# Embedding, attention and experts on one core: the last feature tile of the experts is laid out as a full 64+64 tile and a narrow one whose high and low weights are one stationary operand

## The reference

```python
sg = silu(einsum('bsd,fd->bsf', x, Wsg)); su = einsum('bsd,fd->bsf', x, Wsu)
shared_out = einsum('bsf,df->bsd', sg * su, Wsd)              # shared expert, 704 features
topk_scores, topk_idx = top_k(softmax(logits), 2)             # 8 experts, 2 per token
g = silu(einsum('bsd,efd->bsef', x, Wg)); u = einsum('bsd,efd->bsef', x, Wu)
out_e = einsum('bsef,edf->bsed', g * u, Wd)                   # 352 features per expert
return routed_out + shared_out                                # routed_out weighs out_e by the scores
```

## Time and profile before

| | |
|---|---|
| median of 3 runs | 1667.9 us (1666.66 to 1669.73) |
| profiled execution | 1669.39 us, span 1667.6 us, mean granted TensorE clock 0.984 |
| TensorE busy | 1562.7 us, 94% of the span |
| VectorE busy | 1142.2 us, 68% |
| ScalarE busy | 931.8 us, 56% |
| experts' matmuls | from 719.9 us to the end |

### The profile page before, as it was taken

One profiled execution on the slowest core, in us unless ns is written; L12 is line 12 of the kernel. 1 busy time (PEld: TensorE's weight loads), 2 busy tenths in 40 slices (PEclk: granted clock), 3 DMA queues, 4 the chain that ended last, 5 costly groups with the idle time before them and its releaser, 6 DMA issues.

```text
span 1667.6 us, 34456 instructions
## 1 busy us (share of the span) xinstructions
PE 1562.7 (94%) x11589; PEld 1363.9 (82%) x11652; DVE 1142.2 (68%) x2228; ACT 931.8 (56%) x1902; POOL 528.9 (32%) x517
## 2 busy tenths in 40 slices
PE   2699986999999999879999999999999999999997
PEld 1354544888888888779999999999999999999996
DVE  3588886799999998564434666666666666656665
ACT  4987774687888788532223555555555555522221
POOL 3344445233333422007701222222222221033433
PEclk9999999899999999789999999999999999999999
DMA  9899984122222211131111577777666777543365
GB/s 310 247 317 331 319 267 105 45 59 63 61 65 57 63 51 39 41 129 51 38 50 57 188 246 245 241 246 242 236 237 241 237 238 237 192 152 113 121 217 191
DMA packets 91922, 274.50 MB, mean 165 GB/s; under 512 B 12640, under 2 KB 13152, under 8 KB 91744
## 3 DMA queue, kind: packets, MB, share of 16 engines
q1 hardware_dynamic: 70688, 223.71, 39.3%
q0 software_dynamic: 19072, 45.97, 10.9%
q10 hardware_dynamic: 2112, 4.19, 0.8%
HBM read 228.14 MB, written 45.69 MB: 164 GB/s over the span
## 4 chain that ended last, share of the span: by engine, by line
PE 56%; DMA 1%; DVE 0%; POOL 0%; ACT 0%; issue 0%; POOLq 0%; DVEq 0%
PE up_ps L1338 12%; PE up_ps L1336 12%; PE up_ps L1337 12%; PE down_ps L1336 6%; PE down_ps L1337 6%; PE down_ps L1338 6%; PE xT_ps L1380 2%; DMA comb<-slot_rows,slot_i 0%; DVE H L1286 0%; DMA xr<-x_turned 0%; DVE xT_lo L1203 0%; POOL comb L1138 0%; ACT xT_hi L1153 0%; DVE H L1278 0%; PE route_ps L1332 0%
## 5 line engine op out<-in xcount | busy, mean ns | idle before, releaser
L1336 PE MATMUL up_ps<-xT_hi,w_hi 128*128 128x256 f32 (+1 forms) x1704 | 483.6, 284 | 8.5 <-DVE xT_lo L1203 8.5
L1338 PE MATMUL up_ps<-xT_hi,w_lo 128*128 128x256 f32 (+1 forms) x1704 | 480.8, 282 | 0.0
L1337 PE MATMUL up_ps<-xT_lo,w_hi 128*128 128x256 f32 (+1 forms) x1704 | 478.8, 281 | 0.0
L1336 PEld LDWEIGHTS up_ps<-xT_hi,w_hi 128*128 128x128 f32 (+1 forms) x1704 | 308.0, 181 | 10.0 <-DVE xT_lo L1203 8.6
L1337 PEld LDWEIGHTS up_ps<-xT_lo,w_hi 128*128 128x128 f32 (+1 forms) x1704 | 308.1, 181 | 1.2
L1338 PEld LDWEIGHTS up_ps<-xT_hi,w_lo 128*128 128x128 f32 (+1 forms) x1704 | 308.0, 181 | 0.0
L1208 DVE TENSOR_TENSOR w_lo<-w_stage,w_hi 128x1408 fp32r<-128x1408 f32 (+1 forms) x123 | 201.4, 1665 | 125.0 <-ACT w_hi L1158 124.8
L1130 POOL DMA_INDIRECT xr<-x_rows,slot_tokens x78 | 120.6, 1546 | 441.4 <-PE xT_ps L1380 362.1
L1185 ACT ACTIVATE h_hi<-h 128x256 fp32r<-128x256 f32 (+1 forms) x213 | 89.0, 418 | 240.4 <-DVE h L1301 240.4
L1181 ACT ACTIVATE act_g<-up_ps 128x256 f32<-128x256 f32 (+1 forms) x213 | 79.8, 374 | 182.3 <-PE up_ps L1338 179.6
L288 DVE TENSOR_TENSOR W<-W,norm_ps 128x1000 f32<-128x1000 f32 x128 | 147.2, 1191 | 43.9 <-PE norm_ps L364 35.7
(11 more groups left out here) (184 smaller groups left out, 2738.2 us busy)
## 6 DMA issues: line engine op xcount, KB each, us to landing
W<-table_t SPq DMA_DIRECT2D x32, 2000.0 KB, 14.9
w_stage<-packed SPq DMA_DIRECT2D x80, 704.0 KB, 6.4
w_stage<-packed SPq DMA_DIRECT2D x40, 768.0 KB, 5.2
slot_rows<-y_rows SPq DMA_DIRECT2D x39, 512.0 KB, 6.7
xr<-x_turned SPq DMA_DIRECT2D x32, 512.0 KB, 3.8
x_rows<-x SPq DMA_DIRECT2D x32, 256.0 KB
x_turned<-x2T SPq DMA_DIRECT2D x32, 256.0 KB, 2.5
out<-H SPq DMA_DIRECT2D x32, 256.0 KB, 3.8
```

The source lines that it names most:

```text
L1336: pe.matmul(out, a_hi, b_hi, start=first, stop=False)
L1337: pe.matmul(out, a_hi, b_lo, start=False, stop=False)
L1338: return pe.matmul(out, a_lo, b_hi, start=False, stop=last)
```

## The change

The 96 features of the last tile become 64 ("wide") and 32 ("narrow").

For the 64 wide features, gate and up columns stand side by side and form one stationary operand of 128 columns: 4 steps times 3 matmuls write all 128 partitions of `up_ps[2]`, columns 0 to 255 (gate in partitions 0 to 63, up in 64 to 127).

For the 32 narrow features, the high weights of gate and up (64 columns) and their low weights (64 columns) stand side by side in `w_split` and form one stationary operand of 128 columns. One matmul of it against the high rows gives high times high in partitions 0 to 63 and low times high in 64 to 127 of `up_ps[2]`, columns 256 to 511. The product of the high weights with the low rows is a second matmul with 64 stationary columns, into partitions 0 to 63 of the same place. It is issued between the 128-column ones.

The sum of the two partition halves and the products are then made by more, narrower instructions: ScalarE does silu on 64 partitions, a copy of the other 64 partitions of the narrow part, and a silu on 32 partitions; VectorE adds twice on 32 partitions and multiplies on 64 and on 32. The weights' high and low copies share one tile per buffer, and the low parts of pieces 0 and 1 take two instructions each instead of one. The host packs the columns in the new order; the loads keep their sizes.

The diff goes through the constants, the weight tiles, ScalarE's tiles (`act`), VectorE's low weights and tile 2 (`dve`), and TensorE's tile 2 (`pe`).

```diff
+WIDE, NARROW = 64, 32
+UP_ORDER = ((0, 128), (128, 128), (256, WIDE), (256 + WIDE, NARROW))
+LO_STEPS = (2, 2, 1)
...
-        w_hi = [sb(f"w_hi{i}", [P, PACKED], F32R) for i in range(2)]
-        w_lo = [sb(f"w_lo{i}", [P, PACKED], F32R) for i in range(2)]
+        w_split = [sb(f"w_split{i}", [P, 2 * PACKED], F32R) for i in range(2)]
...
+        up_hi = [u[:, :, 0:2 * ROUTED_F] for u in up_all]
+        up_narrow = [u[:, :, BOTH_FROM:BOTH_TO] for u in up_all]
+        up_lo = [u[:, :, BOTH_TO:K_COLS] for u in up_all]
...
+                    wide = WIDE if j == 2 else f
+                    act.activation(act_g[0:wide, j, :], up_ps[j][0:wide, 0:BLOCK], ACT.Silu).then_inc(silu_done, 1)
+                    if j == 2:
+                        act.activation(act_g[WIDE:P, j, :], up_ps[j][WIDE:P, BLOCK:2 * BLOCK], ACT.Copy).then_inc(silu_done, 1)
+                        act.wait_ge(tail_added, n * 2 + 1)
+                        act.activation(act_g[WIDE:f, j, :], act_g[WIDE:f, j, :], ACT.Silu).then_inc(silu_done, 1)
+                    act.wait_ge(h_done, n * 4 + j + 1 + j // 2)
...
+                    dve.tensor_tensor(up_lo[buffer][:, k, :], whole[:, :, 0:BOTH_FROM], hi[:, :, 0:BOTH_FROM], ALU.subtract).then_inc(w_lo_done[piece], 1)
+                    dve.tensor_tensor(up_narrow[buffer][:, k, 2 * NARROW:4 * NARROW], whole[:, :, BOTH_FROM:2 * ROUTED_F],
+                                      hi[:, :, BOTH_FROM:2 * ROUTED_F], ALU.subtract).then_inc(w_lo_done[piece], 1)
...
+                        dve.tensor_tensor(act_g[WIDE:f, j, :], act_g[WIDE:f, j, :], up_ps[j][0:NARROW, BLOCK:2 * BLOCK],
+                                          ALU.add).then_inc(tail_added, 1)
+                        dve.tensor_tensor(h[WIDE:f, j, :], act_g[f:P, j, :], up_ps[j][NARROW:2 * NARROW, BLOCK:2 * BLOCK],
+                                          ALU.add).then_inc(tail_added, 1)
+                        dve.tensor_tensor(h[0:WIDE, j, :], act_g[0:WIDE, j, :], up_ps[j][WIDE:P, 0:BLOCK], ALU.mult).then_inc(h_done, 1)
+                        dve.wait_ge(silu_done, n * 5 + 5)
+                        dve.wait_ge(tail_added, n * 2 + 2)
+                        dve.tensor_tensor(h[WIDE:f, j, :], act_g[WIDE:f, j, :], h[WIDE:f, j, :], ALU.mult).then_inc(h_done, 1)
...
+                for k in range(KT):
+                    part(up_ps[2][:, 0:BLOCK], wide_at, 2 * WIDE, k, k == 0, k == KT - 1)
+
+                for k in range(KT):
+                    if k:
+                        pe.matmul(up_ps[2][0:2 * NARROW, BLOCK:2 * BLOCK], up_narrow[buffer][:, k - 1, 0:2 * NARROW], xT_lo[odd][:, k - 1, :],
+                                  start=False, stop=False)
+                    if k == KT - 1:
+                        pe.matmul(up_ps[2][0:2 * NARROW, BLOCK:2 * BLOCK], up_narrow[buffer][:, k, 0:2 * NARROW], xT_lo[odd][:, k, :],
+                                  start=False, stop=False)
+                    mm = pe.matmul(up_ps[2][:, BLOCK:2 * BLOCK], up_narrow[buffer][:, k, :], xT_hi[odd][:, k, :], start=(k == 0), stop=(k == KT - 1))
+                mm.then_inc(up_done, 1)
```

More of the change, by code:

```diff
@@ L925, in sem, with staged, hi_part @@
             return ctx.enter_context(nc.semaphore(name))
-        w_hi = [sb(f"w_hi{i}", [P, PACKED], F32R) for i in range(2)]
-        w_lo = [sb(f"w_lo{i}", [P, PACKED], F32R) for i in range(2)]
+        w_split = [sb(f"w_split{i}", [P, 2 * PACKED], F32R) for i in range(2)]
+        K_COLS, BOTH_FROM, BOTH_TO = 4 * ROUTED_F, 2 * ROUTED_F - 2 * NARROW, 2 * ROUTED_F + 2 * NARROW
+        up_all = [w[:, 0:2 * UP_COLS].rearrange("p (k c) -> p k c", k=KT) for w in w_split]
+        up_hi = [u[:, :, 0:2 * ROUTED_F] for u in up_all]
+        up_narrow = [u[:, :, BOTH_FROM:BOTH_TO] for u in up_all]
+        up_lo = [u[:, :, BOTH_TO:K_COLS] for u in up_all]
+        down_hi = [w[:, 2 * UP_COLS:2 * UP_COLS + DOWN_COLS] for w in w_split]
+        down_lo = [w[:, 2 * UP_COLS + DOWN_COLS:2 * PACKED] for w in w_split]
+        def staged(piece):
+            a, b = PIECES[piece]
+            return w_stage[:, a:b] if piece == 2 else w_stage[:, a:b].rearrange("p (k c) -> p k c", k=KT // 2)
+        def hi_part(piece, buffer):
+            return down_hi[buffer] if piece == 2 else up_hi[buffer][:, 2 * piece:2 * piece + 2, :]
         xr = [sb(f"xr{i}", [P, 2, D]) for i in range(2)]
@@ L1043, in load_weights @@
                 for piece, (a, b) in enumerate(PIECES):
-                    after(sp, w_lo_done[piece], w)
+                    after(sp, w_lo_done[piece], w * LO_STEPS[piece])
                     sp.dma_start(w_stage[:, a:b], packed[bass.ds(expert, 1), :, a:b].rearrange("e p c -> (e p) c")).then_inc(stage_in[piece], 16)
@@ L1155, in weights_hi @@
             def weights_hi(w, piece, buffer):
-                a, b = PIECES[piece]
                 after(act, stage_in[piece], w * 16)
-                act.activation(w_hi[buffer][:, a:b], w_stage[:, a:b], ACT.Copy).then_inc(w_hi_done[piece], 1)
+                act.activation(hi_part(piece, buffer), staged(piece), ACT.Copy).then_inc(w_hi_done[piece], 1)
             def take_y(n, kind):
@@ L1341, in up, with part @@
                 pe.wait_ge(xT_lo_done, n + 1)
[L1342 to L1346, removed]
+                for piece in range(2):
+                    pe.wait_ge(w_lo_done[piece], (w + 1) * LO_STEPS[piece])
+                def part(out, at, f, k, first, last):
+                    hi, lo = up_hi[buffer][:, k, at:at + f], up_lo[buffer][:, k, at:at + f]
+                    return three(out, hi, lo, xT_hi[odd][:, k, :], xT_lo[odd][:, k, :], first, last)
+                for j in range(2):
+                    after(pe, h_done, (n - 1) * 4 + j + 1)
                     for half in range(2):
                         for k in range(KT):
-                            c = k * 2 * ROUTED_F + half * ROUTED_F + start
-                            mm = three(up_ps[j][0:f, half * BLOCK:(half + 1) * BLOCK], w_hi[buffer][:, c:c + f], w_lo[buffer][:, c:c + f],
-                                       xT_hi[odd][:, k, :], xT_lo[odd][:, k, :], k == 0, k == KT - 1)
+                            mm = part(up_ps[j][:, half * BLOCK:(half + 1) * BLOCK], j * 2 * P + half * P, P, k, k == 0, k == KT - 1)
                     mm.then_inc(up_done, 1)
+                after(pe, h_done, (n - 1) * 4 + 3)
+                wide_at = 2 * 2 * P
+                for k in range(KT):
[9 more added lines that the diff above has]
+                mm.then_inc(up_done, 1)
             def down(n, odd, w, buffer):
@@ L1432 @@
     packed = np.zeros((n, P, PACKED), gates.dtype)
-    both = packed[:, :, :UP_COLS].reshape(n, P, KT, 2, ROUTED_F)
-    both[:, :, :, 0] = gates.reshape(n, ROUTED_F, KT, P).transpose(0, 3, 2, 1)
-    both[:, :, :, 1] = ups.reshape(n, ROUTED_F, KT, P).transpose(0, 3, 2, 1)
+    both = packed[:, :, :UP_COLS].reshape(n, P, KT, 2 * ROUTED_F)
+    for start, f in UP_ORDER:
+        for half, w in enumerate((gates, ups)):
+            at = 2 * start + half * f
+            both[:, :, :, at:at + f] = w[:, start:start + f].reshape(n, f, KT, P).transpose(0, 3, 2, 1)
     packed[:, :, :UP_COLS] = both.reshape(n, P, UP_COLS)
```

23 lines of the change are left out of this document (14 added, 9 removed).

## The result

The changed kernel takes 1638.78 us (median of 4 runs, 1637.69 to 1641.26) against 1667.28 us for the kernel before in the same session (4 runs, 1664.15 to 1669.73): ratio 0.9836, 95% interval 0.9821 to 0.9851. I had forecast 1702 us, slower. It is faster, and lands on rival 1 (1636 us). The value lies in the wide range of 1633 to 1725 us, which had been drawn down to take in rival 1, and outside the forecast's own 1697 to 1735; the direction was wrong.

The account below looks back on a forecast made before the run. TensorE's row of matmuls was taken as the bound: per block 0.93 us paid less 0.45 saved is +0.48, times 71 is +34 us, other engines 0; forecast 1702 us, own range 1697 to 1735, whole range 1633 to 1725.

Parts of the forecast that it names:

- rival 1: Experts' tile 2: a division of the array by columns changes at no cost; -32 us, 1636 us; 33%.
- What TensorE may pay: Tile 2's alternating 128- and 64-column matmuls: three ways there and back a block at 0.31 us, +0.93 us.
- The upper bound from the earlier trace: Way there and back read from the embedding's row division, with 0.41 us as undisturbed pace: 0.64 us.
- What TensorE loses: Tile 2 goes from 24 matmuls to 20: 0.45 us a block saved, times 71 is 32 us.
- The loop: ScalarE and VectorE work over a B block: grows from 11.36 to 12.8 us, stays covered by TensorE, priced at 0.
- The weights' share: Two more VectorE instructions for the weights' low parts: +0.15 us a block in the ScalarE and VectorE loop.
- Tile 2: Added ScalarE and VectorE instructions there put the high part at 1178.54 instead of 1177.23: +1.31 us in their loop.
- rival 3: Division changes free, but ScalarE and VectorE's loop takes over in B, from 13.1 us a block; 1648 us; 4%.
- wait of 0.3 us: Sign: ScalarE's wait ahead of the result's row tile falls from 2.20 us to this if changes are free.
- a block of 13.1 and distances of 0.12 us: Sign in the profile after: B block length and starts of narrow matmuls that would show division changes are free.
- Rival 2: Tile 2's division changes cost as in the embedding: 1.47 us a block net, +104 us, 1772 us; 7%.
- rival 4: Tile 2: only one direction paid, or half of each, 0.465 us a block; 1669 us, no change; 6% with neighbours.

Follow-up runs that it names:

- rows32: Changed kernel with its four 64-column matmuls using all 128 columns but only 32 of 128 rows; 1793.28 us, ratio 1.031 to the kernel before.
- bf16_cols64: Changed kernel with the four 64-column matmuls reading the upper halves of the same numbers as bf16, still 64 columns; 1779.37 us (one run), kernel before 1737.16.
- full128: Changed kernel with the four 64-column matmuls taking all 128 columns, so nothing divides the array; 1716.67 us, ratio 0.9868 to the kernel before.
- cols32: Changed kernel with the four 64-column matmuls cut to 32 columns, up features' high times low left out; 1639.6 us (one run), kernel before 1666.57.
- before_less4: Kernel before with 20 matmuls instead of 24 in tile 2, nothing else changed; 1631.25 us, ratio 0.9793 to the kernel before.
- loop_plus: Changed kernel with one more VectorE product of 64 x 256 a block into a spare tile; 1731.41 us, ratio 0.9955 to the kernel before.

## Why the prediction was wrong

- **The step that failed is "What TensorE may pay".** I took 0.31 us a way there and back from divisions by rows and put it on one by columns. A number of this size held wherever the change is paid (0.38 by rows here, 0.29 by columns in bf16), but the 64-column matmuls of this kernel are fp32r, and there the group of eight pays nothing (0.934 us against 0.960 undivided) and the block at most 0.017 to 0.026 us for all three ways. None of the rows that I took it from, and the earlier trace rows, was a division by columns, and the term was worth 0.93 x 71 = 66 us, twice the rest of the sum. The upper bound from the earlier trace rows was weak besides: it put the pace of 500-column matmuls, 0.41 us, on ones of 256 columns, which no row shows. The form "128*64" in the built program told that the instruction names a division, not that this one costs.
- The rule that I sided with, "Changing tiling mode (not just tile) drains the TensorE" (the Trainium skill, "TensorEngine Tiling (Array Packing)", "Key Properties"), is borne out by rows32 and bf16_cols64 and not by the changed kernel, full128 and cols32. The measurement decides: for fp32r with all 128 rows no such loss shows in the time. What the array does then, whether it really uses half of the columns, no run shows.
- **"What TensorE loses" was right**: 0.45 us a block forecast, 0.46 measured in tile 2, 0.48 by before_less4 alone. What I missed is that neighbours don't keep their pace: 0.09 to 0.10 us more in tiles 0 and 1 and in `down`, so 0.37 and 0.36 net. 39 x 0.37 + 32 x 0.36 = 26 us, the experts' 26.5.
- **The loop was mis-sized, without a price.** The weights' share held (0.15 forecast, 0.14 measured). Tile 2 was put at +1.31 us and is +1.75: from the low part of tile 1 to the high part of tile 2 it is 1148.79 - 1146.22 = 2.57 us against 1177.23 - 1176.41 = 0.82. I let VectorE's added instructions follow at 0.35 us, a distance read behind a 128-partition low part, and these follow at 0.44 to 0.46, which is 0.3 of the difference; the rest is the first addition, which starts 0.14 later behind ScalarE's copy than I had it. 11.36 + 1.75 + 0.14 = 13.25, and the loop is 13.26 us (ScalarE's copies of the result come 13.16 and 13.36 apart in turn), not 12.8, so rival 3's condition was true: longer than TensorE's 13.19. The slack that the prediction named as over 5 us swallowed it, 0.07 us a block over 39 blocks being under 3; that it did no harm was owed to the count of B blocks, and loop_plus shows what lies beyond. The forecast sign "wait of 0.3 us" came out as no wait at all.
- Of the signs named ahead, a block of 13.1 and distances of 0.12 us stood for rival 1, and both came (13.19, 0.117).
- Rival 2, rival 4: excluded, since no part of the price is paid for a division by columns in fp32r.

## What to carry to other kernels

A price belongs to what was measured: number format and direction of the division included. If the one term that decides the sign comes from rows of another kind, the forecast is a coin toss between the two sums, and a single small kernel that alternates 128 and 64 columns settles it. When matmuls are the bound, cutting their count at the same moving size is worth 0.12 us each at 256 columns, and here a quarter of that went back, most of it to the neighbours' pace. And an engine's share of busy time doesn't tell when it takes over: compare its loop with the block, and count how many blocks the slack lasts.

## What the hardware showed unexpectedly

- Between 128 and 64 (or 32) stationary columns: free in fp32r (the eight narrow matmuls take 0.934 and 0.939 us against 0.960 undivided), 0.29 us there and back with the divided matmul in bf16; between 128 and 32 rows 0.38 us in fp32r.
- A bf16 matmul of 256 columns among fp32r ones keeps their pace, 0.24 us a pair (0.973 against 0.960 us for the eight), though its load is shorter (0.10 us against 0.19).
- Pace differs by 1 to 2% between matmuls of the same form: an `up` matmul goes at 117 to 120 ns, a `down` one at 229 to 233. For `down` it goes with the sequence ahead (4.191 us after the change, 4.144 in full128); for `up` the cause is open.
- VectorE instructions on 32 or 64 partitions last as long as on 128 (0.41 to 0.42 us). In tile 2 they start 0.44 to 0.46 us apart, and the same pair of low part and copy 0.46 apart after the change and 0.34 before; the partitions at which the operands begin may be the reason, which no run tests.
